# Score matmuls over the whole TensorE array, with zero-padded keys and queries

## The reference, cut to what matters

```python
x = x + attention(layernorm(x), wq, wk, wv, wo)   # 16 heads of 16 features
x = x + ffn(layernorm(x), gate_w, up_w, down_w)   # silu(gate) * up, then down; 1024 wide
# attention, of each head, i the query and j the key:
scores = einsum('bihd,bjhd->bhij', q, k) * 16 ** -0.5
scores = where(j - i > 16, -inf, scores)
out = softmax(scores) @ v
```

## Time and profile before

| what | before |
|---|---|
| median of three runs | 530.36 us (530.16 to 531.9) |
| span of the profiled execution, first to last instruction | 529.3 us |
| instructions | 12741 |
| matmuls | 4840 |
| bytes moved by SyncE's DMAs | 43.70 MB |
| mean granted TensorE clock | 0.987 |

### The profile page before, as it was taken

How to read it: one execution, slowest core, us unless ns; L and a number is a source line. 1 busy time by engine, 2 the same in 40 slices (tenths; PEclk the granted TensorE clock), 3 DMA queues, 4 the chain that set the end, 5 groups by cost and what they waited for, 6 DMA issues and landing times.

```text
span 529.3 us, 12741 instructions
## 1 busy us (share of the span) xinstructions
PE 507.1 (96%) x4840; PEld 435.1 (82%) x4840; DVE 425.4 (80%) x944; ACT 364.7 (69%) x536; POOL 211.9 (40%) x255
## 2 busy tenths in 40 slices
PE   7997979999999999999999999999999999999896
PEld 4665757898888898888888898988898888888785
DVE  4585679898898988898998998888988877777853
ACT  3366788676767778686877778686868777775522
POOL 4853345424343342424333352424343333435413
PEclk9898999999999999999999999999999999999999
DMA  8552332214032313131222123133212121300100
GB/s 257 202 179 69 125 101 73 70 50 145 28 113 73 99 62 122 63 120 63 89 84 75 58 81 102 62 100 102 82 60 81 46 78 37 106 2 22 41 21 20
DMA packets 45500, 44.51 MB, mean 84 GB/s; under 512 B 4736, under 2 KB 44544, under 8 KB 45440
## 3 DMA queue, kind: packets, MB, share of 16 engines
q1 hardware_dynamic: 45440, 43.70, 25.0%
HBM read 13.01 MB, written 4.19 MB: 33 GB/s over the span
## 4 chain that ended last, share of the span: by engine, by line
PE 70%; DVE 9%; SPq 9%; DMA 4%; issue 3%; ACT 3%; POOL 1%; POOLq 0%; DVEq 0%; ACTq 0%
PE ring L978 9%; PE ring L979 7%; PE ring L980 7%; PE ring L1056 7%; PE pair L1033 6%; PE pair L1048 6%; PE ring L1087 5%; SPq L670 4%; PE ring L1088 4%; PE ring L1089 4%; SPq L656 3%; DVE M L902 3%; PE ring L971 3%; PE ring L962 2%; PE ring L1076 2%
## 5 line engine op out<-in xcount | busy, mean ns | idle before, releaser
L806 ACT ACTIVATE P<-pair 128x800 f32<-128x800 f32 x128 | 106.4, 837 | 46.6 <-PE pair L1048 37.3
L902 DVE TENSOR_REDUCE M<-pair 128x2 f32<-128x288 f32 (+1 forms) x256 | 133.3, 565 | 2.9 <-PE pair L1033 2.7
L740 POOL TENSOR_TENSOR IN<-GU,IN 128x512 fp32r<-128x512 f32 x64 | 82.6, 1293 | 129.9 <-ACT IN L745 129.4
L745 ACT ACTIVATE pair<-SEED 128x800 f32<-128x800 bf16 x128 | 107.6, 842 | 14.1 <-DVE M L902 10.3
L732 POOL TENSOR_SCALAR_AFFINE_SELECT P<-P 128x448 f32<-128x448 f32 x64 | 37.3, 583 | 120.8 <-ACT P L806 120.8
L978 PE MATMUL ring<-WD,IN 128*128 128x256 f32 x256 | 76.4, 299 | 1.4 <-POOL IN L740 1.1
L1087 PE MATMUL ring<-Y,WGUh 128*128 128x256 f32 x256 | 76.2, 298 | 0.7 <-DVE Y L847 0.4
L1088 PE MATMUL ring<-Y,WGUh 128*128 128x256 f32 x256 | 72.0, 281 | 0.0
L1089 PE MATMUL ring<-Y,WGUl 128*128 128x256 f32 x256 | 71.8, 281 | 0.0
L979 PE MATMUL ring<-WD,IN 128*128 128x256 f32 x256 | 71.6, 280 | 0.0
L980 PE MATMUL ring<-WD,IN 128*128 128x256 f32 x256 | 71.6, 280 | 0.0
(11 more groups left out here) (94 smaller groups left out, 1171.0 us busy)
## 6 DMA issues: line engine op xcount, KB each, us to landing
QM<-QK SPq DMA_DIRECT2D x96, 128.0 KB, 2.1
KS<-QK SPq DMA_DIRECT2D x96, 128.0 KB, 2.1
X<-x SPq DMA_DIRECT2D x32, 256.0 KB, 2.9
out<-X SPq DMA_DIRECT2D x16, 256.0 KB, 2.2
OVERD<-over_down SPq DMA_DIRECT2D x2, 512.0 KB, 7.6
PO<-W SPq DMA_DIRECT2D x16, 48.0 KB, 2.2
P<-wqk SPq DMA_DIRECT2D x2, 256.0 KB, 5.9
QM<-MT SPq DMA_DIRECT2D x32, 8.0 KB
```

The lines of the kernel that those rows point to most:

```text
L745: copy = lambda dst, src: nc.scalar.activation(dst, src, ACT.Copy)
L806: nc.scalar.activation(P[:, g % 2, 2 * (n % 2):2 * (n % 2) + 2, :], pair(what, t, n)[:, :, 0:SW], ACT.Exp, scale=SCALE).then_inc(exp_done, 1)
L902: i = nc.vector.tensor_reduce(out=M[:, t % 2, it, :].rearrange("p (a k) -> p a k", a=2)[:, :, n], in_=pr[:, :, cols], axis=AX.X, op=ALU.ma ...
```

## The change

- Keys and queries get zero-padded copies. `KZ` and `QZ` have for each pair of heads two blocks of columns; block a holds head a in its 64 rows and zeros in the other 64. `QM` and `KS` stay unpadded. An `s1` step is now two matmuls: weights `QM` (128 rows, both heads), streamed `KZ` with 2 x 256 columns, then with 2 x 144. An `sc` step is the same with weights `KS` and streamed `QZ`. The first goes to bank 0 of the pair, the second to bank 1 (`heads_of`); 800 columns lie in a row for seed and exp (`scores`).
- All four are single. `ld` fills `QM` and `KZ` of a half for `s1` with nine DMAs, after the `s1` steps of the sequence before that read it; a new step `lk` fills `KS` and `QZ` for `sc` with nine, after the last `sc` of the sequence before. `QK` becomes double.
- `M` has 128 columns (32 used, the others zero), and `mt` is one 128x128 transpose; `MT` is 32x128, and goes to row 63 of each head in `QZ`.
- POOL's selects are done for each `sc` step, each half as large.
- `Z`, `OT` and `Y` become single; the norms' small tiles (ST, MV, VE, RSTD) double.
- The whole order is new, `START` and all tables; `PERIOD` is 29.4252 in place of 29.3.

The core of the diff:

```diff
-        X, Z = ([sb(f"{n}{i}", [128, TT, D]) for i in range(2)] for n in "XZ")
+        X = [sb(f"X{i}", [128, TT, D]) for i in range(2)]
+        Z = sb("Z", [128, TT, D])
-        QM = sb("QM", [128, 2, NP, S], F32R)
-        KS = sb("KS", [128, 2, NP, S], F32R)
-        QK = sb("QK", [128, 2, 2, 2 * S], F32R)
+        QM, KS = (sb(n, [128, HP, 2, S], F32R) for n in ("QM", "KS"))
+        QZ, KZ = (sb(n, [128, 2, HP, 2, S], F32R) for n in ("QZ", "KZ"))
+        QK = [sb(f"QK{i}", [128, 2, 2, 2, S], F32R) for i in range(2)]
-        M = sb("M", [128, 2, 2, H])
-        P = sb("P", [128, 2, 4, SW])
-        OT = [sb(f"OT{i}", [128, NG, S]) for i in range(2)]
+        M = sb("M", [128, 2, 128])
+        P = sb("P", [128, 2, 2, PS])
+        OT = sb("OT", [128, NG, S])
...
+        def heads_of(pr):
+            return ((pr[:, 0, :].rearrange("p (a c) -> p a c", a=2), S),
+                    (pr[:, 1, 0:2 * W1].rearrange("p (a c) -> p a c", a=2), W1))
+
+        def scores(pr):
+            return pr[:].rearrange("p b c -> p (b c)")[:, 0:PS]
...
                 elif what == "ld":
-                    sp.wait_ge(cleared, 4 if t else 2)
-                    if t >= 2:
-                        sp.wait_ge(sc_made, nth("sc", t - 2, n * HP + HP - 1))
+                    sp.wait_ge(cleared, 2)
+                    if t:
+                        sp.wait_ge(s1_made, nth("s1", t - 1, n * HP + HP - 1))
                     sp.wait_ge(qk_low, nth("qk", t, n))
...
+                    for k, part in enumerate(Q_PARTS):
+                        sp.dma_start(QM[k:128:4, :, n, :].bitcast(F32), QK[t % 2][:, part, 0, n, :].bitcast(F32)).then_inc(
+                            kz_loaded[n], DMA)
+                    for k, part in enumerate(K_PARTS):
+                        for a in range(2):
+                            r = slice(STACK * a, STACK * (a + 1))
+                            sp.dma_start(KZ[STACK * a + k:STACK * (a + 1):4, a, :, n, :].bitcast(F32),
+                                         QK[t % 2][r, part, 1, n, :].bitcast(F32)).then_inc(kz_loaded[n], DMA)
+                elif what == "lk":
+                    sp.wait_ge(cleared, 4)
+                    if t:
+                        sp.wait_ge(sc_made, nth("sc", t - 1, NP - 1))
+                    sp.wait_ge(qk_low, nth("qk", t, 1))
+                    for k, part in enumerate(K_PARTS):
+                        sp.dma_start(KS[k:128:4].rearrange("p j h c -> p j (h c)").bitcast(F32),
+                                     QK[t % 2][:, part, 1].rearrange("p h c -> p (h c)").bitcast(F32)).then_inc(ks_loaded, DMA)
+                    for k, part in enumerate(Q_PARTS):
+                        for a in range(2):
+                            r = slice(STACK * a, STACK * (a + 1))
+                            sp.dma_start(QZ[STACK * a + k:STACK * (a + 1):4, a].rearrange("p j h c -> p j (h c)").bitcast(F32),
+                                         QK[t % 2][r, part, 0].rearrange("p h c -> p (h c)").bitcast(F32)).then_inc(ks_loaded, DMA)
...
+                    dst, value = {0: (KZ, 0.0), 1: (QM, 0.0), 3: (KS, 1.0), 4: (QZ, 0.0)}[n]
+                    nc.gpsimd.memset(dst[:].bitcast(F32), value).then_inc(cleared, 1)
...
                 elif what == "s1":
-                    if n % HP == 0:
-                        pe.wait_ge(qk_loaded[t % 2][n // HP], N_QK * (t // 2 + 1))
-                    pr = pair(what, t, n)
-                    for it, c, w in ((1, W0, S), (0, 0, W0)):
-                        for a in range(2):
-                            r = slice(STACK * a, STACK * a + STACK - 1)
-                            i = mm(pr[:, a, c:c + w], QM[r, t % 2, n, it * 128:(it + 1) * 128], KS[r, t % 2, n, 0:w],
-                                   start=False, stop=it == 0, skip_group_check=True)
+                    h, j = divmod(n, HP)
+                    if j == 0:
+                        pe.wait_ge(kz_loaded[h], N_LOAD * (t + 1))
+                    for it, (o, w) in zip((1, 0), heads_of(pair(what, t, n))):
+                        i = mm(o, QM[:, j, h, it * 128:(it + 1) * 128], KZ[:, :, j, h, 0:w], start=False, stop=True, skip_group_check=True)
                     i.then_inc(s1_made, 1)
                 elif what == "mt":
                     pe.wait_ge(max_done, nth("s1", t, NP - 1))
-                    for it in range(2):
-                        i = turn_to(bk[0:H, it * 128:(it + 1) * 128], M[:, t % 2, it, :], ID[:])
-                    i.then_inc(mt_made, 1)
+                    turn_to(bk[:, 0:128], M[:, t % 2, :], ID[:]).then_inc(mt_made, 1)
                 elif what == "sc":
+                    h, j = divmod(n, HP)
                     if n == 0:
-                        pe.wait_ge(m_loaded[t % 2], N_M * (t // 2 + 1))
-                    pr = pair(what, t, n)
-                    for jt, c, w in ((0, 0, S), (1, S, W1)):
-                        for a in range(2):
-                            r = slice(STACK * a, STACK * (a + 1))
-                            i = mm(pr[:, a, c:c + w], KS[r, t % 2, n, jt * 128:(jt + 1) * 128], QM[r, t % 2, n, S - w:S],
-                                   start=jt == 0, stop=jt == 1, skip_group_check=True)
+                        pe.wait_ge(ks_loaded, N_LOAD * (t + 1))
+                        pe.wait_ge(m_loaded, N_M * (t + 1))
+                    for jt, (o, w) in enumerate(heads_of(pair(what, t, n))):
+                        i = mm(o, KS[:, j, h, jt * 128:(jt + 1) * 128], QZ[:, :, j, h, S - w:S], start=True, stop=True)
                     i.then_inc(sc_made, 1)
```

More of the change, by code:

```diff
@@ L36 @@
 HP = NP // 2
+EDGE = 2 * S
+PS = 2 * SW
 DMA = 16
@@ L182, in spline_tables @@
         rows.reshape(128, -1), powers.reshape(128, INTER), over, over_down, turned.reshape(128, -1))]
-PERIOD = 29.3
+PERIOD = 29.4252
 def steps(table):
[L190 to L195, removed]
[3 rows of a table removed]
-             ("fill", 3, 1, 1, -49.605, 0), ("hot", 3, 1, 1, -45.788, 0), ("fill", 4, 1, 1, -45.146, 0),
[3 rows of a table removed]
-             ("wj", 4, 1, 1, -33.201, 0), ("hot", 4, 1, 1, -29.039, 0), ("hot", 5, 1, 1, -26.819, 0),
[4 rows of a table removed]
[L208 to L211, removed]
[4 rows of a table removed]
@@ L398, in all_steps @@
 def all_steps():
-    out = [(at, what, 0, n) for what, n, at in steps_of_start()]
-    out += [(t * PERIOD + at, what, t, n) for t in range(TURNS) for what, n, at in steps_of_turn(t)]
+    out = [(at, what, 0, n) for at, what, n in steps_of_start()]
+    out += [(t * PERIOD + at, what, t, n) for t in range(TURNS) for at, what, n in steps_of_turn(t)]
     return [i[1:] for i in sorted(out, key=lambda i: i[0])]
@@ L530, in build @@
         GU = sb("GU", [128, 2, 2 * S])
-        Y = [sb(f"Y{i}", [128, 2, 3, S], F32R) for i in range(2)]
+        Y = sb("Y", [128, 2, 3, S], F32R)
+        YT = sb("YT", [128, 2, KB, S], F32R)
         ring = [ctx.enter_context(nc.psum_tensor(f"ring{i}", [128, 512], F32)) for i in range(4)]
@@ L781, in _ @@
                     act.wait_ge(qk_made, nth("qk", t, n))
-                    if t:
-                        act.wait_ge(qk_loaded[(t - 1) % 2][n], N_QK * ((t - 1) // 2 + 1))
-                    copy(QK[:, n, 0, :], bank(what, t, n)[:]).then_inc(qk_high, 1)
+                    if t >= 2:
+                        act.wait_ge(kz_loaded[n], N_LOAD * (t - 1))
+                        act.wait_ge(ks_loaded, N_LOAD * (t - 1))
+                    copy(QK[t % 2][:, 0, :, n, :], halves(bank(what, t, n)[:])).then_inc(qk_high, 1)
                 elif what == "v":
@@ L797, in _ @@
                         act.wait_ge(*emptied(BEFORE["s1", t, n]))
-                    copy(pair("s1", t, n)[:, :, 0:SW], SEED[:].unsqueeze(1).broadcast_to([128, 2, SW])).then_inc(seeded, 1)
+                    copy(scores(pair("s1", t, n)), SEED[:]).then_inc(seeded, 1)
                 elif what == "sc":
@@ L811, in _ @@
                         act.wait_ge(wo_made, nth("wo", t - 1, 0))
-                    copy(OTT[:, 0, :, :], OT[t % 2][:, 0:KB, :]).then_inc(on_high, 1)
+                    copy(OTT[:, 0, :, :], OT[:, 0:KB, :]).then_inc(on_high, 1)
                 elif what == "z2":
                     act.wait_ge(z2_made, nth("z2", t, 0))
+                    if t == 0:
+                        act.wait_ge(permuted, 24 * DMA)
                     if t:
@@ L822, in _ @@
                         act.wait_ge(ws_low, GATE_UP)
-                    if t >= 2 and n == 0:
-                        act.wait_ge(up_made, nth("up", t - 2, 3))
+                    if t and n == 0:
+                        act.wait_ge(up_made, nth("up", t - 1, 3))
                     g = slice(2, 3) if n else slice(0, 2)
-                    copy(Y[t % 2][:, 0, g, :], moments(bank(what, t, n), n)).then_inc(mo_high, 1)
+                    copy(Y[:, 0, g, :], moments(bank(what, t, n), n)).then_inc(mo_high, 1)
                 elif what == "ga":
@@ L849, in _ @@
             nc.vector.memset(HEAT[:], 1.0).then_inc(heat_filled, 1)
```

(27 more changed lines are left out.)

99 lines of the change are left out of this document (54 added, 45 removed), and 297 rows, old and new, of tables (OWN, START, TURN).

## The result

The changed kernel takes 538.7 us (median of 4 runs, 537.72 to 540.97), the kernel before 530.38 beside it: 1.015 times as long (95% interval 1.0121 to 1.0182). The forecast was 519 and faster. In the profiled executions the spans are 539.2 and 529.3 us.

A forecast was written before the change was run, and what follows sets the result against it. TensorE's queue was taken as the steady-part bound: 529.3 - 18.4 (score steps, maxima) + 4 (head) + 3 (single buffers) = 517.9 us span, forecast 519; likeliest case 514 to 524, range 509 to 530.

The forecast's parts named there:

- (5): Single Z, OT and Y, GpSimd's selects and first two fills: charged nothing; late fills would shift the whole head as much.
- Step (1): TensorE's 256 score steps: two full-array matmuls at 0.355 us replace four half-array ones; with av's lost sharing, -13.6 us.
- Step (4): Single QM, KZ, KS, QZ: sc 0 waits behind lk's loads and the maxima; +3 us, bounds 0 and 10.
- Rival C: Slower through single buffers: sc 0 waits for maxima behind lk; from 0.73 us an issue the gain goes; 547 at 0.85; 17%.
- Step (6): Head: SyncE issues 82 DMAs instead of 65, starting at 17.7 us without waiting for the fourth x; +4 us, bounds 0 and +8.
- step (2): Maxima: one full transpose replaces two 16-column ones on TensorE, 0.3 us saved each, 16 times: -4.8 us.
- the gaps in full and 0.22/0.13 within the new step: Sign of being right: full matmuls 0.12 us off before and behind a score step, its own two 0.22 and 0.13 apart.
- `av` paying its gaps alone: TensorE's av runs keep 32-column matmuls and lose neighbours that shared their shape changes; all 43 pay alone: 5 us lost.
- the selects' price: GpSimd's half-size selects: 0.38 and 0.41 us for 224 and 256 elements; 23 us more GpSimd work, charged nothing.
- the end: Behind the last wo: more TensorE work left to cover the chain, so no worse; charged nothing, bounds -3 and +2.
- Rival A: Gaps stay around full-array steps while columns double: a step costs 0.75 us, +83 us, near 610; 3%.
- Rival B: VectorE takes over as bound in the steady part: the turn stays, only the last four gain, about 530; 10%.

The follow-up runs named there:

- fills_first: The changed kernel with GpSimd's first two fills (KZ and QM) placed ahead of all its other work: 531.99 us, ratio 1.0009 to the kernel before.
- mt_next: Changed kernel, first two fills first; on SyncE, x and residual loads and output stores between second-score loads and maxima go behind the maxima: 530.79 us, ratio 0.9988.
- x_first: Changed kernel, KZ fill first on GpSimd, QM fill behind the two RSTDs, first x loaded first, first sequence normalized first: 532.49 us, ratio 1.0022.

## Why the prediction was wrong

**The failing step is (5), on the fills.** It gives a fill of 2048 columns 1.8 us, "one of 4096 about 3.6; the first two end near 15 us, and the first keys are ready at 17.7", warns only of fills that are late, and puts them into the sum at nothing. Duration and end were right (3.51 us, 15.71). What I asked was only who waits for the fills. They were moved beside other work: in the kernel before they are over by 4.5 us, in the new order GpSimd does them straight behind its first subtraction, while VectorE normalizes. VectorE's norm, no reader of the fills, ended with them, and the first keys went out at 24.8. It cost 6.7 us by runs (538.7 to 531.99). Without it the time would still lie above the forecast's range, which ends at 530.

The rest of the 21.3 us between the forecast span, 517.9, and 539.2:

- **Step (1), a price that held a wait.** A new lone step costs 0.366 us where I took 0.355: 2.8 us over 256 steps. Worse, I charged 15 like pairs of old steps at 1.1 us each, 16.5 in all, called part of that a wait for the other PSUM pair, and then let all of it go for 0.355 a step. Priced by the pair that waits for nothing, 0.81 with its gaps, the like pairs carried 15 x (1.1 - 0.81) = 4.4 us of waiting that no new matmul shape removes. In the new kernel it is still there, here between two `s1` steps 1.06 us apart:

```profile
98.91 0.63 PE L998 MATMUL pair<-KZ,QM 128*128 128x512 f32 x2
99.97 0.63 PE L998 MATMUL pair<-KZ,QM 128*128 128x512 f32 x2 [0.42 <-ACT pair L705]
```

  17 runs of just two steps, 13 of them like pairs, take 1.30 us on average, where two steps without a wait take 0.734: 9.6 us of waiting. What they wait for is read from the trace (seeds by ScalarE, loads); no run took these waits away.
- **Step (4), single buffers**, charged at 3 us: TensorE waits 7.9 us for the maxima in 7 places, and in fills_first 5.6 in 6, of which 4.2 after the 150th us. The mechanism was right: with other DMAs out of the chain, in mt_next, the 4.2 became 1.6. Rival C had the right place too, but not the size: in the changed kernel the nine loads took 5.7 to 7.3 us, 0.68 each on average, and only three of 16 sequences lay above the 0.73 from which it was to decide.
- **Step (6), the head**, charged at 4 us for SyncE's chain. Its count of DMAs was right (82, at 58.4 / 82 = 0.71 us each, from a start 7 us late), but taking 24 of them off SyncE gained nothing. The fourth x still stands ahead of the first load of keys, though the step says that the load no longer waits for it. With the fills first, the first output product comes as early as before (72.97 us, 73.06), and the loss shows between it and that of sequence 5. Before, then fills_first:

```profile
73.06:219.28 146.22, 143.38 (x1425) 124.94 (x1425) 129.15 (x289) 108.70 (x161) 57.07 (x71) 1.00 0.25 81
```

```profile
72.97:226.40 153.43, 147.25 (x1271) 128.84 (x1271) 132.78 (x294) 110.20 (x166) 67.64 (x114) 0.99 0.41 135
```

  That is 7.2 us more, where the step's 4 us and the gain of five turns at 1.15 would make it 1.8 less. TensorE idles 6.2 us in it for 2.8. The five sequences behind it take 145.3 us for 146.8.

6.7 + 2.8 + 4.4 and 2.6 more for `sc` 0 (5.6 - 3) make 16.5. Only the first term is from runs; the others are estimates from single places in the traces. Some 5 us stay open. What held: step (2), the maxima (0.60 to 0.12 us with `av` beside), the gaps in full and 0.22/0.13 within the new step, `av` paying its gaps alone (0.20 to 0.23 us ahead of two `av` steps, 0.16 where the old order had a score step there), the selects' price (0.387 and 0.420 us), and the end, which lost nothing (159.2 us from the output product of sequence 10 on, for 163.2). With the DMA share up from 0.25 to 0.41, a load still lands 2.0 to 2.5 us after its issue. Rival A is ruled out: no gaps around full matmuls, whatever the bank. Rival B did not decide: VectorE was busy 26 us of a turn also at 28.6 us a turn.

## What to carry to other kernels

Of work that a new order moves, ask not only who waits for it but what runs beside it: the two fills of GpSimd cost nothing in an idle place, and 6.7 us behind other GpSimd work and beside VectorE's norm, which they held until GpSimd was done. Price an instruction from places where it waits for nothing, and keep the waits as a term of their own: a wait for another engine does not go with the shape of the matmul. And an order and the forms of its steps are priced together: the same new steps are worth 28 us in an order that sets them one by one, and 0.04 us each against old steps laid out in pairs.

## What the hardware showed that was not expected

A TENSOR_SCALAR of 128x256 fp32 from SBUF to SBUF, 0.41 us by itself, that started while GpSimd subtracted or filled lasted until 0.15 us behind the end of GpSimd's work: 6.54 us beside a subtraction and fills of 4096 and 2048 columns, 4.89 us beside the subtraction and two of 2048, 1.86 us beside one fill of 2048, 1.36 us beside the subtraction. The Trainium skill ("SBUF — State Buffer", SBUF: two separate sides) has that VectorE in a 2-port mode and GpSimd take a shared pair of ports as a lock, for a whole instruction, the other being blocked. The blocking agrees; but here the hold went over three instructions of GpSimd, in two kernels. In x_first it ended between a fill and the subtraction behind it, which show no gap either. There the later instruction waits for a semaphore, while the fills have none to wait for; whether that decides was not tried. Not all of VectorE's work is held: in the kernel before, its reductions of the scores (TENSOR_REDUCE, from PSUM) take 0.68 us whether GpSimd is at work or not.
